# One pass of 256 columns for the weighted values of two query tiles, a pair later, and the projections at the end of the pair

## The reference, cut to what matters

```python
q, k, v = to_heads(x @ Wq), to_heads(k), to_heads(v)       # kv = x @ Wkv; 16 heads, 2048 tokens, 64 wide
sim = jnp.einsum('bid,bjd->bij', q, k) * scale
sim = sim + _cope(q, sim, pos_emb)                          # depends on sim near the end of the row
attn = jax.nn.softmax(sim, axis=-1)
out = jnp.einsum('bij,bjd->bid', attn, v)
return out @ Wout + b_out
```

## Time and profile before

| | us |
|---|---|
| median of 3 runs | 2495.25 |
| profiled execution | 2493.37 |
| its span | 2491.5 |
| TensorE matmul busy (PE) | 2340.9 (94%) |
| TensorE weight load busy (PEld) | 1674.2 (67%) |
| VectorE busy (DVE) | 1814.7 (73%) |
| ScalarE busy (ACT) | 1745.9 (70%) |
| GpSimd busy (POOL) | 253.6 (10%) |
| mean granted TensorE clock | 0.991 |

### The profile page before, as it was taken

One profiled execution on the slowest core, in us unless ns is written; L12 is line 12 of the kernel. 1 busy time (PEld: TensorE's weight loads), 2 busy tenths in 40 slices (PEclk: granted clock), 3 DMA queues, 4 the chain that ended last, 5 costly groups with the idle time before them and its releaser, 6 DMA issues. The chain is left out here.

```text
span 2491.5 us, 64093 instructions
## 1 busy us (share of the span) xinstructions
PE 2340.9 (94%) x18687; PEld 1674.2 (67%) x18687; DVE 1814.7 (73%) x4542; ACT 1745.9 (70%) x3767; POOL 253.6 (10%) x417
## 2 busy tenths in 40 slices
PE   7999999999999999999999999999999989999997
PEld 5666666666666666666666666666666656777776
DVE  5888887888888888888888888888888812323231
ACT  5777777777777777777777777777777743444442
POOL 0000000000000000000000000000100001111111
PEclk9999999999999999999999999999999989999998
DMA  2010101010101010101010101010101020101000
GB/s 70 23 38 22 37 21 34 22 38 21 35 22 38 21 35 22 38 21 35 22 38 21 35 22 38 21 37 22 30 13 53 12 63 32 38 25 38 25 27 7
DMA packets 108087, 75.47 MB, mean 30 GB/s; under 512 B 26894, under 2 KB 103823, under 8 KB 107984
## 3 DMA queue, kind: packets, MB, share of 16 engines
q1 hardware_dynamic: 107984, 73.88, 10.8%
HBM read 14.26 MB, written 2.10 MB: 7 GB/s over the span
## 5 line engine op out<-in xcount | busy, mean ns | idle before, releaser
L463 ACT ACTIVATE probsT<-rings 128x512 f32<-128x512 f32 x1024 | 556.4, 595 | 334.9 <-PE rings L615 334.9
L796 DVE TENSOR_REDUCE mx<-Sc 128x1 f32<-128x1024 f32 x512 | 626.8, 1224 | 130.2 <-PE Sc L607 115.1
L615 PEld LDWEIGHTS rings<-ident,probs 128*128 128x128 f32 x4096 | 434.3, 141 | 269.0 <-issue 194.2
L615 PE MATMUL rings<-ident,probs 128*128 128x128 f32 x4096 | 572.9, 283 | 22.1 <-ACT probs L484 1.2
L607 PE MATMUL Sc<-qk,q_now 64*128 64x512 f32 x2048 | 529.6, 615 | 46.8 <-ACT probs L484 26.5
L484 ACT ACTIVATE probs<-Sc,nbias 128x1024 f32<-128x1024 f32 x512 | 566.9, 1121 | 8.6 <-DVE nbias L813 8.6
L629 PE MATMUL out<-probsT,V_now 128*64 128x128 f32 x8192 | 530.0, 277 | 0.0
L629 PEld LDWEIGHTS out<-probsT,V_now 128*64 128x64 f32 x8192 | 439.5, 137 | 58.9 <-issue 45.5
L773 DVE COPY_PREDICATED z<-mask,z 128x224 f32<-128x224 int16 (+5 forms) x768 | 390.8, 509 | 107.6 <-DVE cut L763 33.0
L607 PEld LDWEIGHTS Sc<-qk,q_now 64*128 64x128 f32 x2048 | 188.1, 187 | 232.5 <-issue 231.5
L374 POOL TENSOR_TENSOR prod<-cut,z 128x350 f32<-128x350 f32 x128 | 120.2, 939 | 1577.5 <-DVE z L785 1577.5
(11 more groups left out here) (121 smaller groups left out, 2507.1 us busy)
## 6 DMA issues: line engine op xcount, KB each, us to landing
q_now<-qk SPq DMA_DIRECT2D x256, 64.0 KB, 2.0
xv<-xT SPq DMA_DIRECT2D x113, 128.0 KB, 2.2
q_far<-qk SPq DMA_DIRECT2D x256, 32.0 KB, 1.8
V_now<-V SPq DMA_DIRECT2D x16, 512.0 KB, 3.0
at<-attn SPq DMA_DIRECT2D x16, 512.0 KB, 3.2
probs<-in_x_dram SPq DMA_DIRECT2D x4, 512.0 KB, 5.5
wqk<-in_L_attn_Wq_dram SPq DMA_DIRECT2D x32, 64.0 KB, 2.1
xin<-in_x_dram SPq DMA_DIRECT2D x16, 128.0 KB, 2.8
```

The source lines that it names most:

```text
L463: nc.scalar.activation(probsT[:, u, 4 * s:4 * s + 4, :], ring[k % 2][:, :].rearrange("p (t q) -> p t q", q=P), ACT.Copy).then_inc(slot_out, 1)
L615: last = nc.tensor.transpose(ring[k % 2][:, j * P:(j + 1) * P], probs[:, u, (4 * s + j) * P:(4 * s + j + 1) * P], ident[:, :])
L796: nc.vector.tensor_reduce(mx[:, u, half:half + 1], Sc[:, half * HALF:(half + 1) * HALF], AX.X, ALU.max).then_inc(dve_unit, 1)
```

## The change

The order on TensorE in body g becomes: logits of unit 0; transposes of unit 1 of pair g-1; outputs of both units of pair g-1, 16 tiles of 256 columns; `window`; logits of unit 1; transposes of unit 0 with both turns of pair g-1; `project`; `project_values`. ScalarE copies both halves at once, and takes the two evictions of the projections between the two exponentials of unit 1. VectorE inverts both row sums at once. The slots are renumbered: those of the transposes of unit 0 become 4 to 7, that of `project` 8, that of `project_values` 9. In SyncE's body two waits change; the lines quoted above stay.

```diff
 class Slots:
-    def __init__(self, proj=True):
+    def __init__(self):
         self.last = [0, 1, 2, 3]
-        self.qk, self.values = 4, 5
-        at = 6 if proj else 4
-        self.now = [at, at + 1, at + 2, at + 3]
+        self.now = [4, 5, 6, 7]
+        self.qk, self.values = 8, 9
...
# SyncE
                 if near:
+                    wait_apart(sp, slot_out, base - 1, waited)
                     load_near(g // PAIRS + 1)
                 if head:
-                    wait_apart(sp, out_full, g * 2, waited)
+                    wait_apart(sp, out_full, g, waited)
                     load_values(g)
                 if tile:
                     wait_apart(sp, slot_full, base + Slots().values + 1, waited)
...
# ScalarE
             def body(g, odd, late=False, first=False, proj=True, val=True, far=True, near=True):
...
-                    scale(g - 1, 0)
-                exps(g, 0)
-                if proj:
-                    project(g + PAIRS, not odd, base, at.qk, alone=not val)
-                if val:
-                    values(g, base, at.values)
+                exp_half(g, 0, 0)
+                exp_half(g, 0, 1)
                 if not first:
-                    empty_halves(g - 1, 1)
+                    empty_halves(g - 1)
                 if far:
                     near_tanh(g + 2)
                     near_table(g + 2)
                     steps(g + 2)
                 transposed(0, base, at.now)
+                exp_half(g, 1, 0)
+                if proj:
+                    project(g + PAIRS, not odd, base, at.qk, alone=not val)
+                if val:
+                    values(g, base, at.values)
+                exp_half(g, 1, 1)
                 if not first:
+                    scale(g - 1, 0)
                     scale(g - 1, 1)
-                exps(g, 1)
...
# TensorE
+            def outputs(g, base, slots, empty=True):
+
+                if empty:
+                    pe.wait_ge(halves_out, g)
+                wait_apart(pe, v_in, g // PAIRS * 16 + 16, waited)
+                for t in range(NT):
                     if t % 4 == 0:
                         pe.wait_ge(slot_out, base + slots[t // 4] + 1)
                     half = t % 2 * C
-                    last = nc.tensor.matmul(out[half:half + C, 0:P], V_now[:, token_tile(t), :], probsT[:, u, t, :],
-                                            start=t < 2, stop=t >= NT - 2)
+                    last = nc.tensor.matmul(out[half:half + C, 0:2 * P], V_now[:, token_tile(t), :],
+                                            probsT[:, :, t, :], start=t < 2, stop=t >= NT - 2)
+                last.then_inc(out_full, 1)
...
                 logits(par, 0, 1)
                 if not first:
-                    transposes_and_turn(g - 1, 1, base, at.last, 0, evicted=not second)
-                    outputs(g - 1, 1, base, at.last, tiles=range(FIRST))
-                if proj:
-                    weights_at = (g // PAIRS) * 64 + 128 if val else H * 64 - 16
-                    project(g + PAIRS, not odd, base, at.qk, weights_at, alone=not val)
-                if val:
-                    project_values(g + PAIRS, base, at.values)
-                if not first:
-                    outputs(g - 1, 1, base, at.last, tiles=range(FIRST, NT))
+                    for n in range(4):
+                        transposes(1, base, at.last, n)
+                    outputs(g - 1, base, at.last, empty=not second)
...
-                transposes_and_turn(g - 1, 0, base, at.now, 1, first)
-                outputs(g, 0, base, at.now, empty=not first)
+                for n in range(4):
+                    transposes(0, base, at.now, n)
+                    if n == 1 and not first:
+                        turns_of(g - 1, evicted=not second)
+                if proj:
+                    weights_at = (g // PAIRS) * 64 + 128 if val else H * 64 - 16
+                    project(g + PAIRS, not odd, base, at.qk, weights_at, alone=not val)
+                if val:
+                    project_values(g + PAIRS, base, at.values)
...
# VectorE: one reciprocal of both row sums in place of two; invert(g, 0) at the end of its body goes
```

More of the change, by code:

```diff
@@ L456, in _, with transposed @@
                     steps(1)
-            def transposed(u, base, slots):
-                for s in range(4):
+            def transposed(u, base, slots, sets=range(4)):
+                for s in sets:
                     k = slots[s]
@@ L469, in scale, with empty_halves, exp_half @@
                 h, t = g // PAIRS, g % PAIRS
-                act.wait_ge(rsum_done, g * 2 + u + 1)
-                wait_apart(act, turned, g * 2 + u + 1, waited)
-                nc.scalar.activation(attn[:, t * 2 + u, bass.ds(h * C, C)], turns[:, 0:C], ACT.Copy,
+                if u == 0:
+                    act.wait_ge(rsum_done, g + 1)
+                    wait_apart(act, turned, g + 1, waited)
+                nc.scalar.activation(attn[:, t * 2 + u, bass.ds(h * C, C)], turns[:, u * C:(u + 1) * C], ACT.Copy,
                                      scale=rsum[:, u:u + 1]).then_inc(scaled, 1)
[L475 to L485, removed]
+            def empty_halves(g):
+                act.wait_ge(out_full, g + 1)
+                nc.scalar.activation(halves[:, :, :], out[:, 0:2 * P].rearrange("p (u q) -> p u q", q=P),
+                                     ACT.Copy).then_inc(halves_out, 1)
+            def exp_half(g, u, half):
+                if half == 0:
+                    act.wait_ge(bias_ready, g * 2 + u + 1)
+                cols = slice(half * 2 * BANK, (half + 1) * 2 * BANK)
+                nc.scalar.activation(probs[:, u, cols], Sc[:, cols], ACT.Exp, bias=nbias[:, u:u + 1],
+                                     accum_out=sums[:, u, half:half + 1]).then_inc(exp_done, 1)
             def body(g, odd, late=False, first=False, proj=True, val=True, far=True, near=True):
                 base = slots_before(g, late)
-                at = Slots(proj)
+                at = Slots()
                 if near:
                     positions(g + 1)
-                if not first:
-                    empty_halves(g - 1, 0)
-                if near:
                     distances(g + 1)
@@ L528, in _ @@
             body(G - 1, True, late=True, proj=False, val=False, far=False, near=False)
-            base, at = slots_before(G, True), Slots(proj=False)
-            empty_halves(G - 1, 0)
+            base, at = slots_before(G, True), Slots()
             transposed(1, base, at.last)
+            empty_halves(G - 1)
             scale(G - 1, 0)
-            empty_halves(G - 1, 1)
             scale(G - 1, 1)
@@ L628, in outputs, with turns_of @@
                     half = t % 2 * C
-                    last = nc.tensor.matmul(out[half:half + C, 0:P], V_now[:, token_tile(t), :], probsT[:, u, t, :],
-                                            start=t < 2, stop=t >= NT - 2)
[L631 to L636, removed]
-                if evicted:
[L638 to L647, removed]
+                    last = nc.tensor.matmul(out[half:half + C, 0:2 * P], V_now[:, token_tile(t), :],
+                                            probsT[:, :, t, :], start=t < 2, stop=t >= NT - 2)
+                last.then_inc(out_full, 1)
+            def turns_of(g, evicted=True):
+                pe.wait_ge(halves_out, g + 1)
+                if evicted:
+                    wait_apart(pe, scaled, g * 2, waited)
+                for u in range(2):
+                    last = nc.tensor.matmul(turns[:, u * C:(u + 1) * C], halves[:, u, :], fold[:, :],
+                                            start=True, stop=True)
+                last.then_inc(turned, 1)
             def body(g, odd, par, late=False, first=False, proj=True, val=True, far=True, far_par=None,
@@ L704, in _ @@
             body(G - 1, True, 1, late=True, proj=False, val=False, far=False)
-            base, at = slots_before(G, True), Slots(proj=False)
+            base, at = slots_before(G, True), Slots()
             pe.wait_ge(exp_done, 4 * G)
-            transposes_and_turn(G - 1, 1, base, at.last, 0)
-            outputs(G - 1, 1, base, at.last)
-            turn(G - 1, 1)
+            for n in range(4):
+                transposes(1, base, at.last, n)
+            outputs(G - 1, base, at.last)
+            turns_of(G - 1)
         @block.vector
@@ L814, in bias, with invert @@
                                         negate=True).then_inc(bias_ready, 1)
-            def invert(g, u, used=True):
-                wait_apart(dve, summed, g * 2 + u + 1, waited)
+            def invert(g, used=True):
+                wait_apart(dve, summed, g * 2 + 2, waited)
                 if used:
-                    wait_apart(dve, scaled, g * 2 + u - 1, waited)
-                nc.vector.reciprocal(rsum[:, u:u + 1], rowsum[:, u:u + 1]).then_inc(rsum_done, 1)
+                    wait_apart(dve, scaled, g * 2, waited)
```

(6 more changed lines are left out.)

## The result

The changed kernel takes 3053.34 us (median of 4 runs, 3047.54 to 3058.19) against 2495.16 us: a ratio of 1.223, 95% interval 1.221 to 1.226. Forecast was 2948 us with a range of 2785 to 3000: the direction and the mechanism came out, but the size was 105 us too small, and the measured time lies above the range. The profiled execution took 3056.87 us, 563.5 us more than that of before.

A forecast was written before the change was run, and what follows sets the result against it. TensorE's own order was taken as the bound. Profiled 2493.4 us, plus 329 for SyncE's wait less the gain, plus 140 for the clock, less 16 for outer-loop stretches, gave 2946, as median 2948 us; range 2785 to 3000.

The forecast's parts named there:

- SyncE's wait: Queries issued only after project_values and the tile: TensorE idle 3.84 us before the next logits in each of 112 pairs.
- the allowance of 0.05 us: In SyncE's chain, the time from the landing of the queries to the first matmul, 0.05 us.
- The 0.35 us between the tile's issue and that of the queries: On SyncE's queue, a satisfied wait and the address of the queries, taken as 0.35 us.
- The clock: Granted clock falls behind each idle stretch: 1.25 us a pair, bounds 0 and 1.65, 140 us over 112 pairs.
- The walk without the clock: TensorE's pair summed piece by piece: 8.34 us to unit 1's logits, then 9.99; 18.33 us against 15.39.
- the wide pass: Outputs of both units in one pass of 256 columns: 3.60 us, no time saved per column.
- the second turn: Second turn beside the first, in the transposes of unit 0: 0.12 us more, between 0 and 0.3.
- The 112 pairs: Pairs with a tile: +329 us for the wait less the gain, +140 for the clock, -16 for outer-loop stretches.
- The 16 pairs without a tile: No SyncE wait there; first-half gain stands against the later second exponential: counted 0, within 8 us.
- A clock that holds: Rival: the clock holds, or nearly, despite the idle stretches; 2808 us, chance 0.13.
- The rival of the full price: Clock falls after every wait at the full 1.65 us or more: 2993 us, up to 3020; chance 0.13.
- The third: Rival: queries are there when TensorE asks, no SyncE wait; pair 15.54 us, 2512 us; chance 0.04, half of it slower.

The follow-up runs named there:

- Experiment 1: Changed kernel with load_now (the queries) issued ahead of load_tile and its wait on SyncE, nothing else: 2546.87 us, ratio to before 1.020.
- experiment 4: Kernel before, old order, with one more SyncE wait ahead of load_tile, for the outputs of unit 0: 3071.59 us, ratio 1.231.
- experiment 3: Changed kernel with seven unread matmuls of 256 columns behind project_values in the 112 pairs: 2864.57 us, ratio to before 1.148.
- experiment 5: Kernel of experiment 2 with the outputs made in two passes of 128 columns instead of one of 256: 2459.78 us.
- experiment 2: Changed kernel, load_now ahead of load_tile, both exponentials ahead of projection evictions, a head's first two pairs outside TensorE's inner loop: 2458.05 us, ratio 0.984.
- experiment 8: Changed kernel with the queries issued behind a wait for the last transposes of unit 0: 2593.8 us.

## Why the prediction was wrong in size and right in mechanism

- **SyncE's wait (forecast 3.84 us idle, measured 4.04).** Right. Experiment 1 takes it away and 506 us go with it, experiment 4 adds it to the old order and 576 us come. From unit 1's logits to the next pair it is 10.22 us where the walk had 9.99. Most of this is the allowance of 0.05 us from the landing to the first matmul: second issue 1011.21, landing 2.0 later, matmul at 1013.44, which is 0.23. The 0.35 us between the tile's issue and that of the queries was 0.21 in this pair (1010.67 - 1009.80 - 0.66), 0.39 in the next, and 0.36 on average. The whole difference is 0.23 us a pair, 26 us in all.
- **The clock (forecast 1.25 us a pair, bounds 0 and 1.65; measured 1.73).** This is the step that failed: the term was mis-sized, and its upper bound was wrong. I had priced the low clock by the logits alone, from one row, and counted on the evictions to hide what it does to the transposes ("transposes that wait for evictions hide some more"). For the logits the term was about right, 1.14 us a pair. But the transposes behind them cost another 0.59, and nothing hides it: at full speed the third set waits 0.25 us for an eviction, in the changed kernel the row of all 16, 3.04 us, shows no such wait. By the trace, 1.2 GHz covers 0.54 us of the idle stretch, 2.35 of the logits and 1.45 of the transposes, on average of 111 pairs, and nothing behind them. Measured less forecast is 0.48 us a pair, 54 us.
- **The walk without the clock** was 8.34 us for the first half; experiment 3 shows 8.45. 12 us. The difference is in the logits, which take 1.92 us behind a wait and not 1.81; the 1.99 us of the earlier trace rows beside the 1.89 of the earlier trace rows already told it. The other parts hold: the wide pass 3.60 us as forecast; the second turn nothing (1.35 us from 1005.29 to 1006.64, as with one) where I had 0.12; `project` at its bank's eviction.
- **The 112 pairs** therefore took 2283.9 us against 1740.1, +544 us where 453 were forecast (329 + 140 - 16); 26 + 54 + 12 make up the 91.
- **The 16 pairs without a tile (forecast 0, within 8)** took 234.3 us against 223.1 from the start of the first to the start of the last. There TensorE waits for the first exponential, as in the last row below, and the clock falls in some of them (2.97 us for the logits instead of 2.2). These 11 us, 5.5 us in the stages behind the pairs and 2.9 us in front of them are the other 20 us; the cause of the last two stays open:

```profile
2460.93 2.97 PE L607 MATMUL Sc<-qk,q_now 64*128 64x512 f32 x8 [1.87 <-ACT probs L487]
```

- **The wide pass saves nothing per column.** Right, by experiment 5: 1.7 us between one pass and two, within the spread of each. The rule of the Trainium skill ("TensorEngine Tiling (Array Packing)", section "Instruction Overhead"), read as about 60 cycles on top of each matmul, would have put 0.4 us a pair there; no run here shows them for matmuls of 128 columns or more.
- **The rivals.** A clock that holds (2808 us) is refuted by the clock of 0.89. The rival of the full price (2993, up to 3020 us) came nearest and named the right cause, a clock that stays low beyond the logits; it still gave this too little. The third has no wait of SyncE: it put that kernel at 2512 us, and I expected 2525 of experiment 1, which is that kernel. It gave 2547, so the reordering is a loss even with its main fault mended, by the second exponential it moved back and the 0.34 us within the logits. The sign did turn in experiment 2, and not through the wide pass but through the order on ScalarE.
- **The range.** The clock's price was bounded by one part of the work behind the idle stretch. With half of the transposes' 2.42 us added, which is an estimate, the bound would have been 1.65 + 1.21 = 2.86 us (the dearest pair of the changed kernel cost 2.62, a first half of 11.07 us), and the range would have reached 2948 + 112 x 1.61 = 3128 us.

What stays open is what chooses, among stretches of one length, those that lower the clock; the runs give shares, and no rule.

## What to carry to other kernels

When a step is moved later on one engine, look up who waits for it on a queue in program order, and what stands behind that wait: here an unchanged wait on SyncE carried 506 of the 558 us, and one transfer moved ahead of it gave them back. A long idle stretch on TensorE can be paid twice, and the second payment is spread over the matmuls of several steps behind it; bound it over everything that runs in the time of low clock. Don't take a few stretches that left the clock alone for a rule. If such a wait can't be removed, spare matmuls in it are worth trying.

## What the runs showed of the hardware

- Four isolated stretches of 3.07 to 3.43 us left the granted clock alone in the kernel before, but one of 2.72 us lowered it in experiment 2. Recurring stretches of 4.04 us on average were followed by 1.2 GHz in 109 of 111 pairs, of 3.22 us in 76, of 2.81 us in 57; in experiment 8 none of the 98 under 1.8 us was.
- Seven matmuls whose result nobody reads, in a wait of 4.04 us, kept the clock at 1.00 and made the kernel 189 us (6%) faster.
- Two float32 matmuls in the two column halves cost 0.11 us per 128 columns, at 128 and at 256 columns alike, with twice as many weight loads at 128 (3.65 and 3.60 us for the same work).
